# Cross-attention and quantised feed-forward on one core: row sums ahead of the token quantising, and a period's transposes gathered behind ten matmul units

## The reference, cut to what matters

```
x = x + attn(layernorm(x), ctx, ctx, Wq, Wk, Wv, Wo, bo)   # 16 heads of 64, causal
x = x + ffn(layernorm(x), w_gate, w_up, w_down)
def act_quant(x):                                # one scale per token
    scale = 127 / clip(max(abs(x), -1), 1e-5)
    return clip(round(x * scale), -128, 127) / scale
ffn: gate = silu(act_quant(x) @ wg); up = act_quant(x) @ wu
     return act_quant(gate * up) @ wd            # ternary weights
```

## Time and profile before

| what | value |
|---|---|
| median of 3 runs | 684.04 us (683.62 to 684.99) |
| the profiled execution | 684.53 us, its span 682.6 us |
| busy: PE, DVE, ACT, POOL | 656.3, 551.6, 480.5, 346.2 us |
| granted TensorE clock, mean | 0.982 of full |
| chain that ended last | PE 89%, DVE 4%, issue 3%, POOL 2% |

### The profile page before, as it was taken

One profiled execution on the slowest core, in us unless ns is written; L12 is line 12 of the kernel. 1 busy time (PEld: TensorE's weight loads), 2 busy tenths in 40 slices (PEclk: granted clock), 3 DMA queues, 4 the chain that ended last, 5 costly groups with the idle time before them and its releaser, 6 DMA issues.

```text
span 682.6 us, 17689 instructions
## 1 busy us (share of the span) xinstructions
PE 656.3 (96%) x6626; PEld 497.7 (73%) x6626; DVE 551.6 (81%) x1402; ACT 480.5 (70%) x860; POOL 346.2 (51%) x353
## 2 busy tenths in 40 slices
PE   8899999999999999999999999999999999999763
PEld 5687777777777777787777778777777877777551
DVE  5747988878898787888878888897888889888965
ACT  4686777687777767877776787777678777766623
POOL 0224546454654645465465556546555654554621
PEclk9999999999999999999999999999999999999985
DMA  8188677878777677887777798677778877777741
GB/s 272 47 306 289 184 259 212 284 261 296 228 252 253 234 233 276 293 265 215 245 243 238 263 293 270 221 249 233 235 269 287 268 238 224 251 241 222 274 124 38
DMA packets 89636, 163.59 MB, mean 240 GB/s; under 512 B 40016, under 2 KB 44368, under 8 KB 85584
## 3 DMA queue, kind: packets, MB, share of 16 engines
q1 hardware_dynamic: 89552, 162.48, 72.5%
HBM read 83.02 MB, written 71.30 MB: 226 GB/s over the span
## 4 chain that ended last, share of the span: by engine, by line
PE 89%; DVE 4%; issue 3%; POOL 2%; ACT 1%; DMA 0%; POOLq 0%; DVEq 0%; SPq 0%
PE ps_up L468 8%; PE ps_a L494 7%; PE ps_up L374 5%; PE ps_up L375 4%; PE ps_up L376 4%; PE ps_up L364 4%; PE ps_up L363 4%; PE ps_up L362 4%; PE ps_b L584 4%; PE ps_a L498 4%; PE ps_low L478 4%; PE ps_kv L362 3%; PE ps_kv L364 3%; PE ps_low L376 3%; PE ps_kv L363 3%
## 5 line engine op out<-in xcount | busy, mean ns | idle before, releaser
L665 ACT ACTIVATE v_rows<-ps_up 128x512 f32<-128x512 f32 x126 | 77.3, 615 | 118.4 <-PE ps_up L376 115.6
L1183 POOL TENSOR_TENSOR prob_up<-prob_up,row_rec 128x512 f32<-128x512 f32 x62 | 63.9, 1051 | 112.6 <-DVE row_rec L968 112.6
L1166 POOL TENSOR_TENSOR hid_b<-hid,neg_round 128x512 bf16<-128x512 f32 x62 | 63.1, 1039 | 105.4 <-ACT hid L665 105.4
L1017 DVE SCALAR_TENSOR_TENSOR gated<-gated,ps_g 128x512 f32<-128x512 f32 x58 | 39.6, 683 | 58.1 <-ACT gated L744 58.1
L1171 POOL TENSOR_TENSOR prob_up<-prob_up,row_max 128x1024 f32<-128x1024 f32 x31 | 59.5, 1918 | 53.3 <-DVE row_max L953 53.3
L665 ACT ACTIVATE kp<-ps_up 128x512 f32<-128x512 f32 x120 | 68.8, 600 | 7.9 <-PE ps_up L364 6.9
L494 PEld LDWEIGHTS ps_a<-vp,prob_t 128*32 128x32 f32 x1984 | 55.3, 110 | 18.9 <-issue 17.9
L946 DVE SCALAR_TENSOR_TENSOR prob_up<-ps_up,rs,bias_up 128x512 f32<-128x512 f32 x62 | 43.7, 747 | 26.9 <-PE ps_up L468 26.9
L468 PE MATMUL ps_up<-kp,xt 128*32 128x256 f32 (+1 forms) x768 | 61.7, 454 | 1.0 <-ACT kp L665 1.0
L374 PE MATMUL ps_up<-n_hi,ct_hi 128*128 128x512 f32 x126 | 60.9, 483 | 1.0 <-DVE prob_up L946 0.7
L494 PE MATMUL ps_a<-vp,prob_t 128*32 128x128 f32 x1984 | 59.9, 273 | 0.7 <-ACT prob_t L665 0.7
(11 more groups left out here) (261 smaller groups left out, 1812.9 us busy)
## 6 DMA issues: line engine op xcount, KB each, us to landing
v_mem<-v_rows SPq DMA_DIRECT2D x256, 256.0 KB, 6.8
vp<-v_mem SPq DMA_DIRECT2D x31, 2048.0 KB, 9.1
ct<-in_ctx_t SPq DMA_DIRECT2D x16, 256.0 KB, 9.4
x_res<-in_x SPq DMA_DIRECT2D x16, 256.0 KB, 9.3
xt<-in_x_t SPq DMA_DIRECT2D x16, 256.0 KB, 9.5
out<-x SPq DMA_DIRECT2D x32, 128.0 KB, 5.8
kp<-v_mem SPq DMA_DIRECT2D x2, 1024.0 KB, 7.2
hid_t<-hid_b SPq DMA_TRANSPOSE x62, 3.1
```

Source lines behind the costliest of these rows:

```text
L665: copy = lambda dst, src, **kw: nc.scalar.activation(dst, src, ACT.Copy, **kw)
L1166: p.tensor_tensor(hid_b[:, c, :], hid[0][:, c, :], neg_round[:].broadcast_to([P, F]), ALU.add).then_inc(hb_ready, 1)
L1183: p.tensor_tensor(up[:, half, :, :], up[:, half, :, :], rows(rec[:, 0, :], H, R), ALU.mult).then_inc(normed, 1)
```

## The change

No instruction is added or taken away. On DVE, `sum_rows` and `invert_sums` of quad n now stand ahead of `quantise_x(n-1)`. On PE, ten units instead of eight stand ahead of the first insertion; then come `late`, `down`, the transposes of both upper parts of the probabilities and those of the quantised tokens, unit 10, the transposes of the lower part, the gate and up matmuls of half 0, units 11 to 13, those of half 1, units 14 and 15. ACT follows that order, and both exponentials come one evacuation later. `late` and `down` write bank 6 (ps_g) and the transposed tokens bank 7 (ps_u), the two banks that gate and up write, and the waits are changed accordingly: the first gate matmul now waits for `add_late(n)` and `second_residual(n-2)`.

```diff
-        down_bank = lambda n: banks[4 if n >= LAST - 2 else 5]
+        xqt_place = lambda n: banks[7][:, 0:2 * D] if n < LAST - 2 else out_bank(n)[:, 2 * D:4 * D]
+        down_bank = lambda n: banks[6 if n < LAST - 3 else 5 if n == LAST - 3 else 4]
+        late_bank = lambda n: banks[6 if 0 < n < LAST - 1 else 5]
...
+                if 2 <= n < LAST - 1:
+                    pe.wait_ge(h_step, H_STEPS * (n - 2) + 4)
...
             def transpose_xq(n):
+                if 0 < n < LAST - 2:
+                    pe.wait_ge(h_step, H_STEPS * (n - 1) + 4)
...
+                    if n < LAST - 2:
+                        pe.wait_ge(late_added, n + 2)
+                        if n:
+                            pe.wait_ge(x2_done, 2 * n)
...
                 elif part == 0:
-                    pe.wait_ge(late_added, n + 1 + n // (LAST - 1))
-                    if live(n, 2):
+                    if n == LAST - 1:
+                        pe.wait_ge(late_added, n + 2)
                         pe.wait_ge(x2_done, 2 * (n - 2) + 2)
+                    elif n:
+                        pe.wait_ge(pt_evac, 3 * n)
+                    else:
+                        pe.wait_ge(late_added, 1)
...
-                if live(n, 1):
-                    transpose_xq(n - 1)
-                fill(n, 8)
+                for i in range(8, 10):
+                    fill(n, i)
                 if live(n):
                     late(n)
...
                 if live(n, 2):
                     down(n - 2)
-                if live(n, 1):
-                    gate_up(n - 1, 0)
-                for i in range(9, 12):
-                    fill(n, i)
                 if live(n):
                     prob_transposes(n, 0)
                 if live(n):
                     prob_transposes(n, 1)
                 if live(n, 1):
-                    gate_up(n - 1, 1)
-                for i in range(12, 16):
-                    fill(n, i)
+                    transpose_xq(n - 1)
+                fill(n, 10)
                 if live(n):
                     prob_transposes(n, 2)
+                if live(n, 1):
+                    gate_up(n - 1, 0)
+                for i in range(11, 14):
+                    fill(n, i)
+                if live(n, 1):
+                    gate_up(n - 1, 1)
+                for i in range(14, 16):
+                    fill(n, i)
...
-                if live(n, 1):
-                    quantise_x(n - 1)
                 if live(n):
                     sum_rows(n, 0)
                     sum_rows(n, 1)
                     invert_sums(n)
+                if live(n, 1):
+                    quantise_x(n - 1)
```

More of the change, by code:

```diff
@@ L529, in late @@
                 pe.wait_ge(laterep_done, n // 2 + 1)
+                if 2 <= n < LAST - 1:
+                    pe.wait_ge(h_step, H_STEPS * (n - 2) + 4)
                 col = (2 + last(n)) * D
-                mm(ps_b[:, col:col + D], late_rep[:, n % 2 * QB:n % 2 * QB + QB, :].rearrange("p b i -> p (b i)"), n_sum[:],
+                mm(late_bank(n)[:, col:col + D], late_rep[:, n % 2 * QB:n % 2 * QB + QB, :].rearrange("p b i -> p (b i)"), n_sum[:],
                    start=True, stop=True).then_inc(late_ready, 1)
             def transpose_xq(n):
+                if 0 < n < LAST - 2:
+                    pe.wait_ge(h_step, H_STEPS * (n - 1) + 4)
                 for c in range(2):
                     pe.wait_ge(xq_ready, 2 * n + c + 1)
-                    t = nc.tensor.transpose(out_bank(n)[:, (2 + c) * D:(3 + c) * D], xq[:, c, :], id_sb[:])
+                    t = nc.tensor.transpose(xqt_place(n)[:, c * D:(c + 1) * D], xq[:, c, :], id_sb[:])
                 t.then_inc(xqt_ready, 1)
@@ L578, in prob_transposes @@
                     if n:
-                        pe.wait_ge(xqt_evac, n)
                         pe.wait_ge(x1_done, n)
@@ L733, in take_xq @@
                 act.wait_ge(xqt_ready, n + 1)
-                copy(xq_t[:, :, :].rearrange("p c i -> p (c i)"), out_bank(n)[:, 2 * D:4 * D],
+                copy(xq_t[:, :, :].rearrange("p c i -> p (c i)"), xqt_place(n),
                      bias=-ROUND).then_inc(xqt_evac, 1)
@@ L760, in _ @@
                     exponential(0, 1)
-                for i in range(0, 2):
+                for i in range(0, 3):
                     take(n, i)
@@ L764, in _ @@
                     exponential(n, 0)
-                take(n, 2)
+                take(n, 3)
                 if live(n) and n:
                     exponential(n, 1)
-                for i in range(3, 8):
+                for i in range(4, 8):
                     take(n, i)
@@ L783, in _ @@
                 if live(n, 1):
+                    take_xq(n - 1)
+                take(n, 10)
+                if live(n):
+                    take_probs(n, 2)
+                if live(n, 1):
+                    tanh(n - 1, 0)
+                for i in range(11, 14):
+                    take(n, i)
+                if live(n, 1):
                     tanh(n - 1, 1)
-                take(n, 12)
                 if live(n) and n % 2 == 1 and n // 2 + 2 < GROUPS:
                     round_ctx(n // 2 + 2)
-                for i in range(13, 16):
+                for i in range(14, 16):
                     take(n, i)
-                if live(n):
-                    take_probs(n, 2)
             A, B = LAST - 1, LAST
@@ L1054, in add_late @@
                 col = (2 + last(n)) * D
-                v.scalar_tensor_tensor(o, ps_b[:, col:col + D], unseen[:, n:n + 1], o, ALU.mult, ALU.add).then_inc(late_added, 1)
+                v.scalar_tensor_tensor(o, late_bank(n)[:, col:col + D], unseen[:, n:n + 1], o, ALU.mult, ALU.add).then_inc(late_added, 1)
             for n in PERIODS:
```

## The result

The changed kernel takes 749.86 us (median of 4 runs, 749.01 to 751.74) against 683.93 (four runs, 683.62 to 684.99) for the kernel before: 1.0978 times as long, 95% interval 1.0941 to 1.1016. The prediction was 753, range 718 to 785. The profiled execution has a span of 747.6 us and a granted clock of 0.989.

What follows compares the result with a forecast made beforehand. PE bounds the kernel before; afterwards a chain through DVE, POOL, PE and ACT does, 20.5 us a period, 22.2 with POOL's hold-up. 29 x (22.2 - 19.82) = 69 us more gives 753 us, range 718 to 785.

Steps and rivals of the forecast that it cites:

- PE's own floor: Steady period: PE, busy in all but 0.12 us, alone would bound it at about 19.7 us.
- The second chain: Loop from S through sums, POOL, transposes, gate, tanh and scale_hid to S: 20.5 us a period, 0.7 more than before.
- S: Start of the period's first shift_scores instruction on DVE, from which the forecast counts its times.
- The cover: PE's four units and lower transposes, which hid scale_hid before; without them DVE is late by 0.9 us.
- The hold-up by POOL: DVE's SBUF-to-SBUF TENSOR_SCALARs wait for the running POOL instruction's end; quantising takes 4.4 us instead of 2.75.
- A second term: second_residual and add_late on DVE, for which gate 0 now waits: they add nothing or 0.05 us.
- The size of the hold-up: Quantising beside POOL: lengthens the period from 20.5 us to 22.15, rounded upward to 22.2.
- Sum: 29 x (22.2 - 19.82) = 69 us more, first period and end part taken as nothing: 753 us.
- The clock did not fall: Rival, chance 0.17: PE's idle piece from 11.76 to about 13.1 also lowers the clock; 778 or 803 us.
- No hold-up: Rival, chance 0.07: quantising beside POOL is not slowed; period 20.5 us, 704 us in all.
- only the large ones: Rival, chance 0.10: clip and g_half pass freely beside POOL; period 21.1 us, 722 us in all.
- What was to show it: Signs: PE waits over 1 us for xq, some 29 periods; xn, clip, g_half, xq 0.6 to 1 us.

Runs made afterwards that it cites:

- The PSUM experiment: Changed kernel with the quantising's xn and maximum in PSUM bank 7 and g_half computed from the maximum: 703.95 us, ratio 1.029 to the kernel before.
- The first experiment: Changed kernel with DVE's old order (tokens quantised ahead of the row sums): 800.99 us, ratio 1.1718 to the kernel before.

## Why the prediction was right

- *PE's own floor, about 19.7.* The kernel before with ACT's later exponentials alone runs at 19.77: right within 0.07. The 0.1 us expected from the weight load was 0.05.
- *The second chain, 20.5 without hold-up.* The PSUM experiment has its length and its points: 20.52, with up 0 at 395.31, so gate 0 at about S + 13.08 (forecast 13.1). In the changed kernel gate 0 to gate 1 is 2.54 (2.5) and gate 1 to S 4.91 (4.9). POOL starts at S + 9.13 (9.11). The cover is gone as said: DVE waits for the scores twice instead of 31 times. That this chain is what holds the 20.52 is less well shown than the hold-up: shortening it behind gate 0 by 0.5 us gained nothing until the exponential, a link that it had left out, was moved too, and then 0.17 (20.35).
- *The hold-up by POOL.* Which instructions would be held and where each would end was right: xn S + 10.26 (10.35 forecast), clip 11.21 (11.3), g_half 12.21 (12.3), first xq 12.96 (13.1), second 13.16 (13.3). All are early by 0.1 to 0.14, and that is a mis-sized term: I had let the first xn delay POOL by 0.1. It does not. It is issued at 394.01, POOL at 394.17, only 0.08 behind the reciprocal's end as before, and POOL's instruction keeps its 1.05 us. The Trainium skill, SBUF — State Buffer, section "Who interferes with whom", says of a VectorE instruction in a two-port mode and a GpSimd instruction that whichever issues first holds the shared port pair for its whole instruction, and the other blocks. With POOL first, the trace agrees four times a period. With DVE first it shows no delay, but that is a weak test: by their records the first xn and POOL's instruction overlap by only 0.09 us (394.17 to 394.26).
- *A second term, and some luck.* `add_late` was to add nothing or 0.05. In the periods with the sum over ctx it holds gate 0 up by 0.18 (399.54 to 399.72), so that gate 0 is 1.52 behind the second xq where the sum had 1.4. This error and the early xq partly cancel: 14.68 against 14.75. In the other periods xq is at S + 13.28 (13.45 forecast) and gate 0 at S + 14.63.
- *The size of the hold-up.* Measured, the hold-up costs 1.6 us a period where the sum had 1.7, and the period is 22.12 instead of 22.2.
- *Sum.* 66.8 us in the 29 periods (69 forecast), 0.8 ahead of them, and 2.65 less behind: the ends were taken as nothing, and their net is -1.8 us. Both errors have the same sign and make up the 4 us that the forecast of the added time (69) lies above the 65.0 in the spans.
- *The rivals.* The clock did not fall: PE's idle piece was 1.21 us (1.35 forecast), behind one of 0.25 (the forecast had 0.8 in smaller pieces), and the clock is 1.00 over all periods. The first experiment shows that this rival was near: waits of 1.9 us in the same place brought it down in 28 periods, the one of 1.70 did not. "No hold-up" gave 704 and was measured, where it is true, at 703.95; "only the large ones" is refuted by clip (0.46) and g_half (0.89).
- *What was to show it.* The waits came as listed: 29 for xq of 1.2 us, 29 for prob_up of 0.25 (7.4 in all). The means over all quads are 0.69 us for xn, 0.83 for g_half, 0.56 for xq and only 0.43 for clip, where 0.6 to 1 was said. PE's busy time was to stay near 656 and is 673.1, 20 us more in the steady stretch (594.71 for 574.59), 0.7 a period, for the same number of matmuls. At least 0.4 of it stands beside the waits: the two blocks of upper transposes count 0.61 and 0.66 us, each with a wait behind it, and 0.43 from block to block before. The rest stays open. It made no difference to the period, since PE waits.

## What to carry to other kernels

When a re-ordering takes slack out of one engine's queue, follow every chain that comes back to that engine: here PE with 0.1 us to win bounded the kernel, and DVE with 0.72 us of slack was one edit away from doing so. Before moving small SBUF-to-SBUF instructions of DVE beside a run of POOL instructions, count them: here each TENSOR_SCALAR beside the run could wait out a POOL instruction, even one on two elements, and a PSUM operand at one end freed them (22.12 to 20.52 us a period). And look at how long PE's new wait is in one piece: here 1.2 us cost only itself, 1.9 us cost another 1.2 by the clock.

## What the runs showed of the hardware that was not expected

- The first xn of 0.25 us, issued 0.16 us ahead of POOL's instruction, did not hold it up: POOL starts 0.08 behind its releaser and takes 1.05, as before. The two overlap by only 0.09 us; a longer DVE instruction in front was not seen.
- A held DVE instruction ends 0.08 us (128 elements a partition) or 0.02 to 0.03 us (2 elements) behind POOL's end.
- Not every POOL instruction holds DVE up. In the kernel before, POOL's power (L1125, 128x2) runs from 356.38 to 357.07, and the second xn ends inside it, at 356.76.
- The clock fell behind waits of 1.9 us in otherwise busy periods and not behind one of 1.70 (seen once) or those of 1.21 (28 times); six matmuls without use in that wait made the kernel 33 us faster.
